# The first loads of a fused convolution and quantised FFN: which engine issues them, and in which order

## What is computed

```
ctx  = einsum('nd,od->no', cond_128, c_weight)            # 128x128 by 32x128 -> 128x32
c    = conv1d(x, weight, 9 taps, padding 4, 4 groups of 8 channels)
c    = c + ctx[:, :, None] + bias[None, :, None]
xq   = fake_quant(c, rows);  wq = fake_quant(w, rows)     # 8 bits: max |.| / 127, round
gate = xq @ wq_gate.T ; up = xq @ wq_up.T                 # 512 -> 1376
h    = silu(gate) * up
out  = x + fake_quant(h) @ fake_quant(w_down).T           # 1376 -> 512
```

## Time and profile before

| | us |
|---|---|
| three timed runs: median (lowest, highest) | 282.25 (282.12, 282.53) |
| span of the profiled execution, first to last instruction | 280.7 |
| PE busy in it | 275.1 (98%) |
| DVE busy in it | 243.5 (87%) |
| ACT busy / POOL busy in it | 196.4 / 207.4 |

### The profile page before, as it was taken

One profiled execution on the slowest core, in us unless ns is written; L12 is line 12 of the kernel. 1 busy time (PEld: TensorE's weight loads), 2 busy tenths in 40 slices (PEclk: granted clock), 3 DMA queues, 4 the chain that ended last, 5 costly groups with the idle time before them and its releaser, 6 DMA issues.

```text
span 280.7 us, 5318 instructions
## 1 busy us (share of the span) xinstructions
PE 275.1 (98%) x1862; PEld 153.6 (55%) x1862; DVE 243.5 (87%) x411; ACT 196.4 (70%) x237; POOL 207.4 (74%) x215
## 2 busy tenths in 40 slices
PE   8989999999999999999999999999999999999995
PEld 5978754454564464644444745744444444444443
DVE  0999999999999989799888679789988889888973
ACT  2269999989688886666888836726788886666820
POOL 1478999998969786866888836946778888667732
PEclk9999999999999999999999999999999999999999
DMA  7999923686929999646599992425456763334265
GB/s 268 406 420 419 377 69 71 129 200 171 223 61 221 249 212 238 190 126 187 145 244 296 218 271 77 128 53 128 126 156 163 151 176 98 94 88 124 51 142 187
DMA packets 81721, 51.62 MB, mean 184 GB/s; under 512 B 69664, under 2 KB 70560, under 8 KB 81568
## 3 DMA queue, kind: packets, MB, share of 16 engines
q1 hardware_dynamic: 81264, 50.84, 66.5%
q10 hardware_dynamic: 432, 0.46, 0.5%
HBM read 25.99 MB, written 8.39 MB: 122 GB/s over the span
## 4 chain that ended last, share of the span: by engine, by line
PE 85%; DMA 6%; DVE 4%; SPq 3%; issue 1%
PE bank L1305 52%; PE bank L1329 26%; PE bank L1207 6%; DMA h_mem<-w_gate_up 6%; DVE d_max L855 2%; SPq L352 1%; DVE gu_max L838 1%; SPq L340 1%; PE bank L1344 1%; DVE sg_mem L910 0%; PE bank L1231 0%; SPq L343 0%; DVE sg_mem L989 0%; SPq L329 0%; DVE gu_scale L845 0%
## 5 line engine op out<-in xcount | busy, mean ns | idle before, releaser
L1305 PE MATMUL bank<-wgu_t,xq_mem 128*128 128x512 bf16 (+1 forms) x768 | 154.8, 357 | 0.0
L544 POOL TENSOR_TENSOR sg_mem<-sg_mem,gu_scale_row 128x512 f32<-128x512 f32 (+1 forms) x96 | 110.9, 1162 | 36.3 <-ACT sg_mem L702 36.2
L1305 PEld LDWEIGHTS bank<-wgu_t,xq_mem 128*128 128x128 bf16 x768 | 73.7, 98 | 73.2 <-DVE h_mem L923 1.6
L702 ACT ACTIVATE sg_mem<-sg_mem,x_scale 128x512 f32<-128x512 f32 (+1 forms) x96 | 62.7, 672 | 30.0 <-DVE sg_mem L910 29.5
L1329 PE MATMUL bank<-wd_t,hq_mem 128*128 128x512 bf16 (+1 forms) x341 | 78.2, 379 | 0.0
L923 DVE SCALAR_TENSOR_TENSOR h_mem<-bank,x_scale,sg_mem 128x512 f32<-128x512 f32 (+1 forms) x96 | 65.7, 691 | 8.9 <-POOL sg_mem L544 8.2
L910 DVE TENSOR_TENSOR sg_mem<-bank,gu_scale_row 128x512 f32<-128x512 f32 (+1 forms) x96 | 59.7, 626 | 9.4 <-PE bank L1305 9.2
L707 ACT ACTIVATE h_mem<-h_mem,h_inv 128x1376 f32<-128x1376 f32 (+1 forms) x32 | 45.3, 1419 | 28.2 <-DVE h_inv L831 28.2
L1329 PEld LDWEIGHTS bank<-wd_t,hq_mem 128*128 128x128 bf16 (+1 forms) x341 | 33.4, 98 | 39.6
L928 DVE TENSOR_REDUCE h_max<-h_mem 128x1 f32<-128x1376 f32 x31 | 48.8, 1576 | 0.0
L715 ACT ACTIVATE hq_mem<-h_mem 128x1376 bf16<-128x1376 f32 (+1 forms) x32 | 42.0, 1314 | 0.2
(11 more groups left out here) (71 smaller groups left out, 175.2 us busy)
## 6 DMA issues: line engine op xcount, KB each, us to landing
xo_mem<-x SPq DMA_DIRECT2D x24, 256.0 KB, 3.0
out<-xo_mem SPq DMA_DIRECT2D x24, 256.0 KB, 2.2
hq_mem<-w_gate_up SPq DMA_DIRECT2D x7, 512.0 KB, 10.9
slab_taps<-x_slabs SPq DMA_DIRECT2D x6, 512.0 KB, 5.5
slab<-x_slabs SPq DMA_DIRECT2D x6, 512.0 KB, 8.7
slab_taps<-w_down SPq DMA_DIRECT2D x3, 688.0 KB, 14.2
h_mem<-w_gate_up SPq DMA_DIRECT2D x4, 512.0 KB, 15.8
slab_taps<-x SPq DMA_DIRECT2D x1, 2048.0 KB, 9.8
```

The lines of the kernel that those rows point to most:

```text
L544: pool.tensor_tensor(s, s, gu_scale_row[:, 1, at:at + n], ALU.mult).then_inc(silu_scaled, 1)
L702: act.activation(s, s, ACT.Silu, scale=x_scale_of(i)).then_inc(silu_done, 1)
L1305: last = pe.matmul(bank[n % 2][:, 0:cols], xq_t[:, g, k, P * c:P * (c + 1)], wgu_t[:, m, k, at:at + cols], start=(k == 0), stop=(k == KT - 1))
```

## The change

SP issues piece 2 between pieces 1 and 3, so that every SP issue after piece 1 has one more issue ahead of it. ACT no longer issues piece 2, and its other DMA, `small_sb`, stands behind the trial of Silu and no longer ahead of it. Sizes, semaphores, waits and the order on PE, DVE and POOL stay as they are.

```diff
@@ block.sync
+            def load_second():
+                words = slice(FIRST * N, SECOND * N)
+                sp.dma_start(slab0[:, words], x_slabs[0, :, words]).then_inc(second_in, 16)
...
             load_first()
+            load_second()
             load_third()
             load_pair(1)
             load_pair(2)
@@ block.scalar
-            words = slice(FIRST * N, SECOND * N)
-            act.dma_start(slab0[:, words], x_slabs[0, :, words]).then_inc(second_in, 16)
+            act.activation(silu_trial[:, :], ones[:, 0:1], ACT.Silu)
             act.dma_start(small_sb[:, :], cond_ctx_bias).then_inc(small_in, 16)
-            act.activation(silu_trial[:, :], ones[:, 0:1], ACT.Silu)
```

## The result

The changed kernel takes 284.0 us (median of 19 runs, 282.49 to 285.4); the kernel before, run beside it, 282.43 (19 runs). The ratio is 1.005, with a 95% interval of 1.0038 to 1.0063: slower by 1.6 us in the medians. The forecast was no change, 282.2, with a range of 281.6 to 282.9.

What follows compares the result with a forecast made beforehand. Bound: bytes up to the ninth weight tile, landing at 26.01, then DVE and PE's chain from 38.84. Tile arm 0, DVE arm 0.05 us earlier but hidden; span 280.7 plus 1.55 gives 282.25, stated as 282.2, range 281.6 to 282.9.

Steps and rivals of the forecast that it cites:

- Piece 3 and all later SP issues come one issue later: SP's issues at the start: 0.47 us later each, ninth weight tile still landing at 26.01 by bytes; cost 0.
- the queue is always filled: Bulk transfers behind piece 3: 512 KB issued every 0.47 us while the DMA needs 1.29 us for each.
- Upper bound 0.3: DMA stream from 1.70 to 2.50 us: its changed filling could move the ninth weight tile, at most 0.3 us loss.
- The two arms: Entry stage: bytes up to the ninth weight tile decide; piece 1, first pair, ctx, shift, DVE's list has 0.3 us to spare.
- Piece 1 alone: Start of the DMA: piece 1 lands 0.3 to 0.4 us earlier, about 3.4; first pair begins at most 0.1 earlier.
- `small_sb` behind the trial: ACT's start: issue at 2.26, 1.08 us later, landing about 6.0 against 6.56 wanted; cost 0.
- Rival A: At L1279, ctx operands land too late and DVE waits; slower, 282.6 to 284.1, middle 283.4; chance 0.10.
- Rival B: First pair on PE: piece 2 or 3 late, a gap keeps PE slow; 282.9 to 283.7; chance 0.06.
- by bytes it is there 0.5 us before it is wanted: First pair on PE: argument against a gap, piece 2 arriving 0.5 us before PE wants it.
- Rival C: DMA start: stream fills earlier, ninth weight tile lands 0.3 to 0.6 us earlier; 281.7 to 281.9; chance 0.11.
- the bytes arrive as before: DMA stream: by the skill's rule a second issuing engine saves only sequencer time, so arrival is unchanged.

Runs made afterwards that it cites:

- e10: Kernel before plus a spare 256-byte SP issue behind pair 2, so pairs 1 and 2 keep their times; 282.49 us, ratio 1.0004.
- e7: Kernel before with SP waiting ahead of piece 3 for a GpSimd mark at about 1.6 us, no extra DMA; 283.36 us, ratio 1.0035.
- e14: Another profiled execution of the changed kernel, nothing altered; span 281.6 us against 280.7 before.
- e15, e13: Another profiled execution of the changed kernel, nothing altered; span 281.8 us against 280.7 before.
- e16: Another profiled execution of the changed kernel, nothing altered; span 281.9 us against 280.7 before.
- e1: The changed kernel measured again, nothing altered; 283.33 us, ratio 1.0027 to the kernel before.
- e3: Kernel before with only the ACT order changed: Silu trial ahead of small_sb, piece 2 still on ACT; 282.63 us, ratio 0.9999.
- e6: Against the kernel before, pieces 2 and 3 both on ACT, small_sb its third issue, pair 1 on SP at 1.19; 283.37 us, ratio 1.0033.
- e2: Changed kernel with the ACT order taken back (small_sb ahead of the trial), piece 2 still on SP; 284.27 us, ratio 1.0057.
- e5: Changed kernel with pieces 2 and 3 merged into one 448 KB DMA on SP, pair 1 at 1.66; 282.79 us, ratio 1.0015.
- e12: Against the kernel before, blocks 2 to 8 as one DMA on ACT, then small_sb; pair 1 on SP at 1.19; 282.53 us, ratio 1.0021.

## Why the prediction was wrong

- **The failing step** is "Piece 3 and all later SP issues come one issue later", priced at 0 with the reason "the queue is always filled". I compared a rate, 0.47 us per issue against 1.29 us of DMA time for 512 KB, and this is right behind pair 2 (e10: 1.0004). It is wrong for the first two microseconds, where the pieces are small: 736 KB in all, used up at about 4.25, and pair 1, issued 0.46 us later, was not flowing freely then. The stream fell to 133 to 250 GB/s (433 before), and the kernel took 0.9 to 1.6 us more. The lateness alone does it: e7, with a wait in place of the DMA, lost 0.9. The sum of bytes issued against bytes moved, which I made for `small_sb`, I did not make for the stream.
- **The bound on it** was too narrow. "Upper bound 0.3" was for the filling between 1.70 and 2.50, where nothing changed (100 GB/s in both). The trough is worth 0.6 us of stream in the first profile, up to 1.3 in e14 (0.51 MB short by 7.00), and a wait in PE comes on top.
- **The two arms** were not the whole. That PE's chain carries any delay of the entry to the end was right. But in the first profile neither arm, as I had drawn them, was late: the ninth weight tile landed at 26.0, and DVE's list began at 6.95, 0.24 earlier than before. The delay came by a third way that I had not priced, the slabs behind the first pair: I followed only piece 3 into it. Pair 1's slab had landed at 6.0, wanted at 7.0, and landed at 7.2; pair 3's landed 1.3 us later than before and is on the chain. In e15 and e16 the chain goes over pair 1's slab, in e1, e13 and e14 over a weight tile.
- **Piece 1 alone** landed after 2.7 us and not 3.0, as forecast, and PE could not use it: its first load is at 3.85 again, and not at the 3.75 of the forecast.
- **`small_sb` behind the trial** was issued at 0.81 and not at 2.26. Cost 0 was right (e3), the reason wrong: the issue does not wait for the table load. Rival A did not happen in this change; e6 shows its price where the piece comes at 1.67 on a full DMA.
- **Rival B**, a gap in the first pair with the low clock behind it, was given 0.06. The gap came in three of six executions of the changed kernel, by piece 3 (0.2, 0.6 and 0.4 us in e1, e13 and e16), each time with a granted clock of 1.00 behind it. With 0.50 behind it, it came in e2 only (1.9 us), and there 282.9 to 283.7 was too small: 286.28. e7 has the low clock too, but behind a gap ahead of the second pair, which rival B does not name. Among the first 19 runs a lowered mean clock shows in two, 284.87 and 285.4 us. My reason against it, "by bytes it is there 0.5 us before it is wanted", rests on the same full stream.
- **Rival C** did not happen: the stream has 100 GB/s from 1.70 to 2.50 in both kernels.
- **The rule of the Trainium skill** on which the prediction drew: "DMA: Bandwidth & Descriptors", section "Issuing engines are not separate DMA queues", says that a second issuing engine saves only the sequencer's time. e5 agrees as to queues between 4.25 and 5.25 (406 GB/s from one). But my conclusion, that the bytes arrive as before, does not follow from it: the time saved, one slot of 0.47 us, is what the change gave away, and e7 measures a delay of SP by about as much (pair 1 at 2.03 and not 1.66) at 0.9 us.

What stays open: why the packets of a transfer issued at 2.1 are slow until 5.0 to 5.25, some 3 us after its issue, where piece 1 has its first bytes 1.0 us after its own and a full stream after 1.8; and why the trough's depth varies from 133 to 250 GB/s between executions of one kernel. That pair 1's time of issue makes the trough is shown; the mechanism in the DMA is not.

## What to carry to other kernels

While a DMA stream starts, count for each moment the bytes issued against the bytes moved; a comparison of rates holds only once a backlog is there. In such a start the issue slots of an engine (0.47 us each here) are scarce: a second engine for a small piece, or two pieces merged, keeps the first big transfer where it is. Getting it out earlier still gained nothing here (e6, e12), as the small pieces then came late. Follow every slab behind the moved issue, not only the one moved. And where a transfer slips in front of PE, price the wait and the clock behind it together.

## What the runs showed of the hardware that I had not expected

- A DMA issue on ACT does not wait for the table load or the activation listed ahead of it: issue at 0.81, load from 0.74 to 2.02 (changed kernel); issue at 1.25, load from 1.18 to 2.46 in e3.
- The clock's rise is not at a fixed time, by the spacing of the loads. The first pair's 36 loads took 2.10 us in e7, 58 ns each, and 3.45 us in e5, 96 ns each, both without a recorded wait inside the pair and with a granted clock of 1.00. At a granted clock of 0.50, in e2 from 9 to 12 us, 29 loads took 2.94 us, 101 ns each, near the 103 of the earlier trace rows. So the column does not show the low level of the start; the spacing does.
- In the trough the packets are slow, more than the engines are idle: in e7 the share is 0.91 at 207 GB/s, in the changed kernel 0.86 at 203, in the kernel before 1.07 at 433.
- In the trough SP's own issues are held longer: 0.67 and 0.65 us at 4.53 and 5.24 in the changed kernel, 1.13 at 4.06 in e2, where 0.43 to 0.46 is usual.
